# The last tile of a sparse graph-attention layer, gathered and scored in three parts, and four masks built later

## What is computed

```python
h = jnp.maximum(_layernorm(x, axis=-1), 0.0)
x = x + _L0_gnn_ref(h, adj, L0_gnn_Wq, L0_gnn_Wk)
h = jnp.maximum(_layernorm(x, axis=-1), 0.0)
x = x + _L1_gnn_ref(h, adj, L1_gnn_W, L1_gnn_b_W, L1_gnn_a_vec, L1_gnn_b_a)
...
# L0: cosine-normalised Q and K of h, att = softmax over neighbours of Kn @ Qn.T
prop_fea = att @ features
# L1: h = node_features @ W.T + b_W; e = leaky(h @ a1 (row) + h @ a2 (column) + b_a)
scores = jnp.where(adjacency_matrix > 0, e, jnp.float32(NEG_INF))
h_prime = jax.nn.softmax(scores, axis=1) @ h
```

## Time and profile before

| | before |
|---|---|
| median of 3 runs | 1599.63 us (1599.62 to 1599.75) |
| profiled execution, its own time | 1598.47 us |
| its span | 1596.6 us |
| busy: PE, DVE, ACT, POOL | 1102.4, 993.2, 970.0, 1101.7 us |
| adjacency loads end, in the span | about 806 us |
| first gather of the second layer | 899.86 us |

### The profile page before, as it was taken

One profiled execution on the slowest core, in us unless ns is written; L12 is line 12 of the kernel. 1 busy time (PEld: TensorE's weight loads), 2 busy tenths in 40 slices (PEclk: granted clock), 3 DMA queues, 4 the chain that ended last, 5 costly groups with the idle time before them and its releaser, 6 DMA issues.

```text
span 1596.6 us, 22567 instructions
## 1 busy us (share of the span) xinstructions
PE 1102.4 (69%) x6257; PEld 873.3 (55%) x6257; DVE 993.2 (62%) x4076; ACT 970.0 (61%) x2806; POOL 1101.7 (69%) x1137
## 2 busy tenths in 40 slices
PE   6887778887777788787765366556656665656666
PEld 4663555555554565555565355545555555555655
DVE  6977679887898787888875243444344434444444
ACT  5663778778877787877789544444444444444432
POOL 2247677677777777777676377777777777777774
PEclk9997889998999888999877677787777777787777
DMA  9998999999999999999922122222222222222221
GB/s 366 424 395 340 411 376 404 410 406 366 391 407 408 356 405 405 407 395 407 381 54 54 39 57 60 60 61 59 61 60 60 59 61 60 59 61 59 61 61 44
DMA packets 90988, 359.56 MB, mean 225 GB/s; under 512 B 23909, under 2 KB 36584, under 8 KB 58088
## 3 DMA queue, kind: packets, MB, share of 16 engines
q1 hardware_dynamic: 49128, 277.05, 43.0%
q0 software_dynamic: 34816, 72.49, 17.7%
q10 hardware_dynamic: 6912, 8.52, 1.5%
HBM read 345.25 MB, written 12.72 MB: 224 GB/s over the span
## 4 chain that ended last, share of the span: by engine, by line
POOL 44%; issue 17%; DMA 16%; PE 9%; ACT 8%; DVE 5%; SPq 0%; ACTq 0%; POOLq 0%; DVEq 0%
POOL arena L519 19%; DMA arena<-in_adj_dram 15%; POOL arena L514 13%; POOL arena L940 7%; POOL arena L946 5%; ACT prod L1166 3%; PE ps L990 3%; PE ps L1015 3%; ACT diag L1185 1%; DMA arena<-tab,idx_shared 1%; PE ps L971 1%; PE ps L1027 1%; ACT R L1136 1%; ACT R L1138 1%; ACT R L1134 1%
## 5 line engine op out<-in xcount | busy, mean ns | idle before, releaser
L940 POOL DMA_INDIRECT arena<-tab,idx_own x320 | 329.3, 1029 | 142.2 <-issue 90.8
L519 POOL DMA_INDIRECT arena<-tab,idx_own x320 | 302.2, 944 | 97.5 <-issue 97.5
L990 PE MATMUL ps<-arena,fold 128*128 128x512 fp8e4 x1024 | 279.7, 409 | 95.1 <-DMA arena<-in_adj_dram 94.5
L535 PE MATMUL ps<-ident,arena 128*128 128x128 f32 x704 | 147.4, 385 | 209.4 <-DMA arena<-tab,idx_shared 209.4
L514 POOL DMA_INDIRECT arena<-tab,idx_shared x224 | 214.2, 956 | 96.8 <-issue 68.0
L946 POOL DMA_INDIRECT arena<-tab,idx_shared x224 | 217.3, 970 | 68.3 <-issue 68.3
L535 PEld LDWEIGHTS ps<-ident,arena 128*128 128x128 f32 x704 | 130.2, 281 | 222.5 <-DMA arena<-tab,idx_shared 222.5
L587 ACT ACTIVATE arena<-arena,negm 128x517 f32<-128x517 f32 (+1 forms) x64 | 56.8, 887 | 277.2 <-DVE negm L653 277.2
L990 PEld LDWEIGHTS ps<-arena,fold 128*128 128x128 bf16 x1024 | 91.0, 99 | 242.1 <-DMA arena<-in_adj_dram 134.5
L1166 ACT ACTIVATE prod<-prod,arena 128x128 f32<-128x128 f32 x544 | 210.3, 391 | 0.4 <-ACT s_all L402 0.4
L643 DVE SCALAR_TENSOR_TENSOR arena<-ps,s_all,arena 128x512 f32<-128x512 f32 (+1 forms) x112 | 66.9, 634 | 205.3 <-PE ps L535 205.3
(11 more groups left out here) (186 smaller groups left out, 2432.2 us busy)
## 6 DMA issues: line engine op xcount, KB each, us to landing
arena<-in_adj_dram SPq DMA_DIRECT2D x256, 1024.0 KB
arena<-tab,idx_own POOLq DMA_INDIRECT x640
arena<-tab,idx_shared POOLq DMA_INDIRECT x448, 2.6
tab<-arena ACTq DMA_DIRECT2D x16, 260.0 KB, 7.6
tab<-tw ACTq DMA_DIRECT2D x32, 130.0 KB
res<-in_x_dram SPq DMA_DIRECT2D x8, 512.0 KB, 11.7
out_dram<-arena SPq DMA_DIRECT2D x64, 64.0 KB, 1.6
prod<-in_L_gnn_Wq_dram SPq DMA_DIRECT2D x1, 64.0 KB
```

The source lines that it names most:

```text
L519: pool.indirect_dma_start(out=GO[q][:, s, :], out_offset=None, in_=tab1, in_offset=bass.IndirectOffsetOnAxis(ap=idx_own[:, t, s:s + 1], ax ...
L535: last = nc.tensor.matmul(T_ps[c // 4][:, c % 4 * P:(c % 4 + 1) * P], GS[h % 2][:, first + c, D:D + 1].to_broadcast([P, P]), ident[:, :], ...
L940: pool.indirect_dma_start(out=G[q][:, s, :], out_offset=None, in_=tab0, in_offset=bass.IndirectOffsetOnAxis(ap=idx_own[:, t, s:s + 1], axi ...
L990: last = nc.tensor.matmul(keys_ps[t % 2], fold[:, PIECE_BITS * f + b, :], ring8[m % RING][:, b * WORDS:(b + 1) * WORDS], start=False, stop ...
```

## The change

The masks of tiles 0 to 3 leave the first layer's loop; `lists_scalar` now builds 0 to 7 at its head. For tile 63, POOL gathers the 3 chunks first, then own slots 0 to 2, then own slots 3 and 4, the latter with a semaphore of their own. DVE, ACT and PE treat the tile in these three parts: products, scores and exponentials by part, diagonals in two calls. ACT's tail does each part earlier than the scores, exponential and diagonals stood before. The sums are the same.

```diff
--- before.py
+++ after.py
@@ -415,7 +415,7 @@
         s_free, s_n, s_off = sem("keys_free"), sem("spill_counts"), sem("spill_offsets")
         s_took = sem("spill_offsets_taken")
         s_R, s_E, s_Eev, s_idx = sem("owner_mask"), sem("owner_rows"), sem("owner_rows_copied"), sem("shared_idx_written")
-        s_own = sem("own_idx_written")
+        s_own, s_last = sem("own_idx_written"), sem("last_own_gathered")
 
         s_g = [[sem(f"{tag}_gathered_{q}") for q in range(GR)] for tag in ("own", "spill")]
         s_prod, s_red, s_ex = sem("l0_products"), sem("l0_scores"), sem("l0_weights")
@@ -445,6 +445,7 @@
         s_R1 = sem("l1_owner_mask")
         s_go = [*s_g[0], *s_g[1][0:GR1 - GR]]
         go_before = [16 * K * len(range(q, T, GR)) for q in range(GR)]
+        go_before[(T - 1) % GR] -= 16 * (K - 3)
         go_before += [16 * sum(len(GIVEN[t % QT]) for t in range(q, T, GR)) for q in range(GR)]
         s_gs = [[sem(f"l1_spill_gathered_{q}_{u}") for u in range(QT)] for q in range(2)]
         s_T, s_sc, s_ex1, s_tr1 = sem("l1_edge_scores"), sem("l1_scores"), sem("l1_exp"), sem("l1_weights_transposed")
@@ -593,7 +594,7 @@
                     last = nc.scalar.activation(diag[p][:, s, :], ident[:, :], ACT.Copy, scale=sc[p][:, s:s + 1])
                 last.then_inc(s_dg1, 1)
 
-            for t in range(QT, AT1):
+            for t in range(AT1):
                 masks1_scalar(act, t)
             for t in range(T + 1):
                 if t >= 1:
@@ -931,22 +932,31 @@
                 pool.wait_ge(s_edge, 32)
                 for p in range(HR):
                     pool.wait_ge(s_tst[p], 16 * (NB // HR))
-                for t in range(T):
-                    q = t % GR
-                    if t >= GR:
-                        pool.wait_ge(s_pv, t - GR + 1)
+                def gather_own(t, first, end, landed):
                     pool.wait_ge(s_own, t // 2 + 1)
-                    for s in range(K):
+                    for s in range(first, end):
                         pool.indirect_dma_start(
-                            out=G[q][:, s, :], out_offset=None, in_=tab0,
+                            out=G[t % GR][:, s, :], out_offset=None, in_=tab0,
                             in_offset=bass.IndirectOffsetOnAxis(ap=idx_own[:, t, s:s + 1], axis=0),
-                            bounds_check=None).then_inc(s_g[0][q], 16)
+                            bounds_check=None).then_inc(landed, 16)
+
+                def gather_shared(t):
                     pool.wait_ge(s_idx, t + 1)
                     for c in GIVEN[t % QT]:
                         pool.indirect_dma_start(
                             out=Gc[:, (C * (t // QT) + c) % CR, :], out_offset=None, in_=tab0,
                             in_offset=bass.IndirectOffsetOnAxis(ap=idx_shared[:, t // QT, c:c + 1], axis=0),
-                            bounds_check=None).then_inc(s_g[1][q], 16)
+                            bounds_check=None).then_inc(s_g[1][t % GR], 16)
+
+                for t in range(T - 1):
+                    if t >= GR:
+                        pool.wait_ge(s_pv, t - GR + 1)
+                    gather_own(t, 0, K, s_g[0][t % GR])
+                    gather_shared(t)
+                pool.wait_ge(s_pv, T - GR)
+                gather_shared(T - 1)
+                gather_own(T - 1, 0, 3, s_g[0][(T - 1) % GR])
+                gather_own(T - 1, 3, K, s_last)
                 either(pool, lambda e: None, lists_gpsimd)
 
             @block.tensor
@@ -1028,6 +1038,20 @@
                     for s in range(K):
                         last = nc.tensor.matmul(pv_ps[p][:, 0:ROW], diag[t % DR][:, s, :], G[q][:, s, :], start=False,
                                                 stop=s == K - 1)
+                    last.then_inc(s_pv, 1)
+
+                def weighted_last(t):
+                    p, q, n = t % 2, t % GR, PAIRED[t % QT]
+                    pe.wait_ge(s_W, paired(t + 1))
+                    pe.wait_ge(s_fin, t - 1)
+                    for j in range(n):
+                        v, s, e = shared(t, SPAN[t % QT][0] + j)
+                        nc.tensor.matmul(pv_ps[p][:, 0:ROW], W[p][j], Gc[:, e, :], start=j == 0, stop=False)
+                    for part, (a, b) in enumerate(((0, 3), (3, K))):
+                        pe.wait_ge(s_dg, t + 1 + part)
+                        for s in range(a, b):
+                            last = nc.tensor.matmul(pv_ps[p][:, 0:ROW], diag[t % DR][:, s, :], G[q][:, s, :], start=False,
+                                                    stop=s == K - 1)
                     last.then_inc(s_pv, 1)
 
                 def offsets_after(i):
@@ -1083,7 +1107,7 @@
                 weighted(T - 2)
                 second.tensor_tr(pe, PAIRS - 3)
                 second.tensor_pr(pe, PAIRS - 3)
-                weighted(T - 1)
+                weighted_last(T - 1)
                 for i in (PAIRS - 2, PAIRS - 1):
                     second.tensor_tr(pe, i)
                     second.tensor_pr(pe, i)
@@ -1243,25 +1267,49 @@
                         second.scalar_h(act, (t - 8) // 2)
                     if t + 3 < T:
                         masks(t + 3)
-                    if t == T - 4:
-                        act.wait_ge(s_piece, PIECES * T)
-                    if t >= T - 4:
-                        masks1_scalar(act, t - T + 4)
+
+                def last_scores(t, first, end, n):
+                    act.wait_ge(s_prod, made(t) + n)
+                    for s in range(first, end):
+                        if s < K:
+                            norm_of = G[t % GR][:, s, RN:RN + 1]
+                        else:
+                            norm_of = Gc[:, shared(t, GIVEN[t % QT][s - K])[2], RN:RN + 1]
+                        nc.scalar.activation(prod[t % 2][:, s, :], prod[t % 2][:, s, :], ACT.Copy, scale=norm_of,
+                                             accum_out=score[t % 2][:, s:s + 1]).then_inc(s_red, 1)
+
+                def last_exps(t, first, end, had, n):
+                    act.wait_ge(s_red, red(t) + had)
+                    if n == 1:
+                        act.wait_ge(s_W, paired(t - 2))
+                        act.wait_ge(s_dg, t - 3)
+                    nc.scalar.activation(weight[t % 4][:, first:end], score[t % 2][:, first:end], ACT.Exp).then_inc(s_ex, 1)
+
+                def last_diags(t, first, end, n):
+                    act.wait_ge(s_ex, t + n)
+                    act.wait_ge(s_pv, t - DR + 1)
+                    for s in range(first, end):
+                        last = nc.scalar.activation(diag[t % DR][:, s, :], ident[:, :], ACT.Copy, scale=weight[t % 4][:, s:s + 1])
+                    last.then_inc(s_dg, 1)
 
                 second.scalar_hT(act, PAIRS - 5)
                 weights(T - 2)
                 second.scalar_h(act, PAIRS - 4)
                 second.scalar_rows(act, PAIRS - 5)
+                last_scores(T - 1, K, slots(T - 1), 1)
+                last_exps(T - 1, K, slots(T - 1), 3, 1)
                 second.scalar_root(act, PAIRS - 3)
                 second.scalar_hT(act, PAIRS - 4)
-                scores(T - 1, 0, K)
+                last_scores(T - 1, 0, 3, 2)
+                last_exps(T - 1, 0, 3, 6, 2)
+                last_diags(T - 1, 0, 3, 2)
                 second.scalar_h(act, PAIRS - 3)
                 second.scalar_rows(act, PAIRS - 4)
-                scores(T - 1, K, slots(T - 1))
-                exps(T - 1)
+                last_scores(T - 1, 3, K, 3)
+                last_exps(T - 1, 3, K, 8, 3)
+                last_diags(T - 1, 3, K, 3)
                 second.scalar_hT(act, PAIRS - 3)
                 second.scalar_root(act, PAIRS - 2)
-                diags(T - 1)
                 second.scalar_rows(act, PAIRS - 3)
                 second.scalar_h(act, PAIRS - 2)
                 second.scalar_hT(act, PAIRS - 2)
@@ -1528,14 +1576,21 @@
                         link.add(nc.vector.tensor_scalar(none_all[:, :], cnt_all[:, :], 0.0, None, ALU.is_equal))
                         link(nc.vector.tensor_scalar(some_all[:, :], cnt_all[:, :], 0.0, None, ALU.is_gt))
 
+                def last_own_products(t, first, end, landed, n):
+                    dve.wait_ge(landed, n)
+                    nc.vector.tensor_tensor(prod[t % 2][:, first:end, :], G[t % GR][:, first:end, 0:D],
+                                            repeat(owner[:, t, 0:D], end - first), ALU.mult).then_inc(s_prod, 1)
+
                 second.vector_stats(dve, link, PAIRS - 4)
                 spill_weights(T - 3)
                 finish(T - 5)
+                dve.wait_ge(s_red, red(T - 2))
+                spill_products(T - 1)
                 spill_weights(T - 2)
-                own_products(T - 1)
+                last_own_products(T - 1, 0, 3, s_g[0][(T - 1) % GR], go_before[(T - 1) % GR])
                 finish(T - 4)
                 second.vector_stats(dve, link, PAIRS - 3)
-                spill_products(T - 1)
```

(1 more changed line is left out.)

## The result

The changed kernel takes **1591.49 us** (median of 18 runs, 1588.14 to 1595.94). In the same comparison the kernel before took 1597.39 us (18 runs, 1592.18 to 1602.16, the three shown earlier among them). The ratio is 0.9958, 95% interval 0.9948 to 0.9968: faster by 6.7 us, 5.1 to 8.3.

What follows compares the result with a forecast made beforehand. The second layer runs at POOL's gather rate; its first gather waits for the last store, behind ACT's drain, then DVE and PE. Tile 63's sums start 5.45 us earlier: 1599.63 - 5.45 = 1594.2 us, range 1592.9 to 1597.2.

Steps and rivals of the forecast that it cites:

- The level of before: Whole kernel before: median taken as 1599.63 us, 1.16 us above the profiled execution, from which 5.45 us was subtracted.
- The sum for ACT: First layer's drain: L386 of pair 29 starts at 879.31 instead of 883.55 us; masks -5.37, waits -1.08, diagonals +1.47, exponentials +0.74.
- Both waits: ACT's two waits in the first layer's drain, 0.85 and 0.23 us, would go: 1.08 us.
- From L386 to the sums: PE's projection of pair 29 stands ahead of tile 63's sums, which start 1.24 us after L386.
- All that follows up to the store: From tile 63's sums on PE to the last store: durations unchanged, everything 5.45 us earlier.
- Gathers: POOL's eight gathers for tile 63, in parts: cost nothing, landing 3 to 5 us before ACT reaches them.
- Second-layer masks: ACT builds eight masks instead of four, 6.85 us more, fitting by 1.0 us before tile 0's exponential; cost nothing.
- Rival 1: End of first layer: stores wait for each other, 4.05 us each, 0.9 us lost, 1595.1 us; chance 0.16.
- rival 2's first case: PE slow all through tile 61 in the drain: 1.4 us added, 0.6 counting, 1594.8 us; chance 0.10.
- Rival 3: PE never speeds up between 871 us and the last store: 1601.8 us; chance 0.05 together with other losses.
- rival 2's second case: PE slow in tile 62 too: 2.5 us more, about 1597.6 us; chance 0.13, shared with parts not helping.

Runs made afterwards that it cites:

- the masks' kernel: Kernel before with only the masks of tiles 0 to 3 moved, tile 63 left whole: 1592.17 us, ratio 0.9958 to before.
- the parts': Changed kernel with the four masks put back, so only tile 63 in three parts: 1597.48 us, ratio 0.9998 to before.
- own_first4: Changed kernel with tile 63's chunks gathered behind its own slots, as before: 1595.04 us, ratio 0.9987 to before.

## Why the prediction was right, and where it was wrong

**The level of before, wrong.** The step that failed is in the sum: "the median lies 1.16 us above it, 1599.63 - 5.45". I took the median of three runs, within 0.13 us of each other, as the level. The next runs went from 1592.18 to 1602.16 us, and the median of 18 is 1597.39, 2.24 us lower: most of the 2.7 us by which the forecast missed. Four sessions at 1.6 ms gave before 1597.39, 1599.01, 1599.72 and 1598.15 us. My range had no term for it: downwards only 1.3 us for the mechanism. With 1597.39 - 5.45 = 1591.9 the same sum would have been 0.45 us off.

**The sum for ACT, right in kind, 0.3 us short.** 4.53 us were measured for 4.24. The exponentials were priced at 0.37 us each; the first of the three adds 875.67 - 875.05 - 0.39 = 0.23 us, since `lnv` follows 0.11 us behind its start. That accounts for half. The rest is in the steps: the rows of pair 28 started 1.72 us after L370 in before (879.16 to 880.88) and 0.77 in after (878.86 to 879.63), so the wait that was priced at 0.85 cost 0.95, and the step behind the store of pair 27 is 0.06 us shorter (0.37 against 0.43). The diagonals ahead of L386 came as priced. Both waits vanished as forecast. The reason given for the first, that ACT has 2 us more to do there, is borne out: in the masks' kernel, which lacks them, the wait stays, and grows by PE's clock.

**From L386 to the sums, right.** 1.06 us were measured for 1.24; before had 2.45. The releaser is the projection, as forecast.

**"All that follows up to the store" unchanged, wrong by 0.25 us.** From the sums' start to the last store before took 9.55 us, after 9.30, the masks' kernel 8.87, the parts' 8.81 and `own_first4` 8.78. The work is the same. The 0.25 us are the first six records of the sums (0.75 us to the next in before, right behind a wait, and 0.67 in after) and the last pair's transposes (0.60 and 0.44 us). The last pair's four projection records took 1.24 us in before and 1.23 in after, but 0.71 in the masks' kernel, behind the same waits of 2.35 and 0.56 us. Two single profiles can thus differ by 0.7 us in this stretch through PE's clock alone, and of the 6.17 us at the store I count 5.9 to the change.

**Gathers, "Cost nothing, cover 3 to 5 us", right in that they cost nothing, and only with the chunks first.** The covers were 2.7, 1.9 and 3.0 us, the forecast somewhat too wide. The other order costs 3.6 us, which the prediction never weighed, and an estimated 1.5 us of that come from a landing of 3.1 us where it had 1.62.

**Second-layer masks, right.** They fit by 0.67 us where 1.0 was forecast.

**Rival 1, absent.** The store of pair 28 was issued at 880.17 us and the rows of pair 29 started at 883.55, released by PE and not by the store: it had landed within 3.4 us. The last landing took 3.83 us to POOL's release in after, and 3.2 us pass from the last store's issue to the first gather in the masks' kernel. Taking nothing was right; the six profiles have 3.1 to 4.6 us from the last store's issue to the first gather (before 4.31). The Trainium skill's 2.0 us ("DMA: Bandwidth & Descriptors", Anatomy of one DMA) is for a DMA that GpSimd issues; this store is issued by ACT, and no run shows its fixed part.

**Rivals 2 and 3, half there.** Windows of after at 874 to 876 and 876 to 878 us, in the columns of the earlier trace rows:

```profile
874.00:876.00 2.00, 1.99 (x10) 2.00 (x11) 0.95 (x3) 1.67 (x9) 0.87 (x1) 0.50 0.51 133
876.00:878.00 2.00, 2.00 (x16) 2.00 (x16) 1.15 (x6) 1.94 (x11) 0.00 (x0) 0.82 0.01 4
```

The clock rose in tile 61's sums, as in before, and tiles 62 and 63 ran at 2.4 GHz although PE waited 1.49 us between them. In the masks' kernel all of tile 61 ran at 1.2 GHz, which is rival 2's first case: it was priced at 1.4 us and took 1.5, all that the wait of 2.36 us has over the 0.85 of before. So the rival was real and didn't come in the profile of the change. The Trainium skill ("TensorE: Matmul & The Clock Gate", HAM oscillation) says that waits between short bursts put PE back to half rate. The example there waits several microseconds at a time; the 1.49 us here are less, so that the prediction went further than the page when it called this rival the case by that rule. For the last pair, behind a wait of 2.35 us, PE was back at half rate in before and after, and not in the masks' kernel. Rival 3 didn't come: tiles 62 and 63 ran at 2.4 GHz. One slip in the sums: rival 2's second case is 1594.8 + 2.5 = 1597.3 us, not 1597.6, and rival 3 with it 1601.5.

**What stays open.** Why executions of one kernel differ by 10 us. The six profiles at 1.6 ms bound it: the last fold of adjacency starts between 805.2 and 809.6 us, the stretch from the last store to the first gather varies from 3.1 to 4.6 us, and the second layer from 696.7 to 700.6 us. These together could make most of it, but no run isolated one. Open too is what decides when PE's clock rises or falls in this drain, which was worth 1.5 us in the masks' kernel.

## What to carry to other kernels

A base of three runs that agree closely isn't a level: give the forecast as a difference, and give the range a term for how far single executions spread. When two halves of a change don't add up, compare the durations of the same records before you call it an interaction: here 3.9 and 0.5 us against 5.9 was PE's clock in one profile. Measure the simplest half alone, too: moving four masks took as much off the kernel's time as the whole change. And where a tile is split into parts, cost each order of its gathers; the order that wasn't taken would have cost more than the parts gain.

## What the hardware showed unexpectedly

- The same program took 1.6 ms in some sessions and 1.9 ms in others, one chip number showing both, with PE idle for 465.9 instead of 61.3 us ahead of one group of matmuls (and 14.6 instead of 209.4 ahead of another), and ratios between two kernels that differ between sessions by 2.5%.
- Behind equal waits of 2.35 and 0.56 us, PE's four records of one projection took 1.24 or 0.71 us. Behind nearly equal histories, the sums and the projection of tile 61's turn ran at 1.2 GHz to the end in one profile and not in another, 1.5 us apart.
- The last gather of the first layer landed 3.1 us after its issue ended in two kernels; three others in before and after, whose landing released DVE, took 1.6 us.
- 544 gathers, with no wait among them, took 3.7 us longer in one execution than in another.
